# Convolution from stacked taps on half the array, softplus as one ScalarE activation, slots set anew

## The reference

```
xn = layernorm(x) * (1 + scale) + shift
x_in, z = split(xn @ in_proj_w.T)                  # 1024 channels each
u  = silu(causal_conv(x_in, 4 taps per channel) + conv_b)
dt_r, B, C = split(u @ x_proj_w.T)                 # 64, 16, 16
dt = softplus(dt_r @ dt_proj_w.T + dt_proj_b)
A  = -exp(A_log)
for t: h = h * exp(dt[t] * A) + (dt[t] * u[t]) * B[t];  y[t] = sum over 16 states of h * C[t]
y  = (y + u * D_param) * silu(z);   x + gate * (y @ out_proj_w.T)
```

## Time and profile before

| | |
|---|---|
| median of 3 runs (lowest to highest) | 2305.18 us (2304.23 to 2309.43) |
| profiled execution, its own time | 2300.15 us |
| its span, mean granted TensorE clock | 2298.4 us, 0.964 |
| busy PE, DVE, ACT, POOL | 2129.7, 2043.7, 1607.3, 1776.1 us |
| first scan to last scan | 65.5 to 1804.6 us |
| chunks 1 to 7, length | 215.9, 216.6, 218.1, 215.5, 218.4, 218.0, 214.3 us |

### The profile page before, as it was taken

One profiled execution on the slowest core, in us unless ns is written; L12 is line 12 of the kernel. 1 busy time (PEld: TensorE's weight loads), 2 busy tenths in 40 slices (PEclk: granted clock), 3 DMA queues, 4 the chain that ended last, 5 costly groups with the idle time before them and its releaser, 6 DMA issues. The chain is left out here.

```text
span 2298.4 us, 30570 instructions
## 1 busy us (share of the span) xinstructions
PE 2129.7 (93%) x10240; PEld 1396.4 (61%) x10240; DVE 2043.7 (89%) x2255; ACT 1607.3 (70%) x3120; POOL 1776.1 (77%) x1047
## 2 busy tenths in 40 slices
PE   8789989988998999899979988998977899999999
PEld 3355555555655555555545555555545588888878
DVE  4999999999999999999999999999999766666666
ACT  4677877887787778777877887777656355566655
POOL 0697899999999999999999999999999521233325
PEclk9999999999998999999999999998978999999999
DMA  7611321151114111421331141114001201121113
GB/s 241 244 38 51 123 103 47 53 177 46 51 51 166 51 55 43 179 92 51 115 111 47 51 165 56 42 53 173 33 28 53 93 28 35 33 63 60 40 56 129
DMA packets 86138, 191.20 MB, mean 83 GB/s; under 512 B 8349, under 2 KB 11677, under 8 KB 85982
## 3 DMA queue, kind: packets, MB, share of 16 engines
q1 hardware_dynamic: 85982, 189.25, 24.8%
HBM read 171.91 MB, written 17.30 MB: 82 GB/s over the span
## 5 line engine op out<-in xcount | busy, mean ns | idle before, releaser
L1473 POOL TENSOR_TENSOR arena<-arena 128x1024 f32<-128x1024 f32 x512 | 1201.2, 2365 | 114.4 <-ACT arena L628 112.0
L1065 DVE TENSOR_TENSOR_SCAN arena<-ps,arena 128x512 f32<-128x512 f32 x1024 | 1240.1, 1257 | 15.2 <-ACT ps L628 12.4
L628 ACT ACTIVATE ps<-arena 128x512 f32<-128x512 f32 x1087 | 717.3, 676 | 274.3 <-DVE arena L1065 188.1
L341 PEld LDWEIGHTS ps<-keep,arena 128*128 128x128 f32 x4096 | 491.2, 147 | 266.2 <-POOL arena L1473 133.6
L341 PE MATMUL ps<-keep,arena 128*128 128x128 f32 x4096 | 548.5, 284 | 98.0 <-POOL arena L1473 91.7
L1050 DVE TENSOR_TENSOR arena<-ps,arena 128x1024 f32<-128x1024 f32 x407 | 491.0, 1206 | 25.9 <-PE ps L341 23.4
L280 PE MATMUL ps<-arena 128*128 128x512 f32 x1024 | 469.3, 604 | 18.4 <-issue 17.6
L280 PEld LDWEIGHTS ps<-arena 128*128 128x128 f32 x1024 | 189.8, 195 | 219.9 <-issue 219.4
L628 ACT ACTIVATE arena<-ps 128x512 f32<-128x512 f32 (+1 forms) x393 | 198.4, 538 | 124.9 <-PE ps L280 64.4
L1440 POOL TENSOR_TENSOR arena<-arena 128x1024 f32<-128x1024 f32 x105 | 248.0, 2362 | 15.1 <-PE ps L341 15.1
L628 ACT ACTIVATE arena<-arena 128x2 f32<-128x2 f32 (+4 forms) x662 | 238.3, 365 | 26.4 <-POOL arena L1417 7.5
(11 more groups left out here) (151 smaller groups left out, 2693.6 us busy)
## 6 DMA issues: line engine op xcount, KB each, us to landing
arena<-scr_bc SPq DMA_DIRECT2D x128, 512.0 KB, 7.2
arena<-in_inT SPq DMA_DIRECT2D x184, 256.0 KB, 2.7
arena<-in_x SPq DMA_DIRECT2D x17, 512.0 KB, 3.8
scr_x<-arena SPq DMA_DIRECT2D x32, 256.0 KB, 2.0
arena_b<-scr_x SPq DMA_DIRECT2D x16, 512.0 KB, 3.6
arena_c<-scr_x SPq DMA_DIRECT2D x32, 256.0 KB, 2.9
out<-arena_c SPq DMA_DIRECT2D x32, 256.0 KB, 2.1
arena<-in_x SPq DMA_DIRECT2D x30, 256.0 KB, 3.4
```

The source lines that it names most:

```text
L341: last = e.matmul(YP[:, 128 * q:128 * q + 128], hb[G % R][:, i, 128 * q:128 * q + 128], ident, start=(g == 0 and i == 0 and q == 0), stop= ...
L628: return e.activation(o_, i_, f, **kw)
L1065: e.tensor_tensor_scan(H, DA[s % 4], H, h0, MUL, ADD).then_inc(v_sc)
L1473: e.tensor_tensor(H, H, Ct[:, GN * g:GN * g + GN, :], MUL).then_inc(g_w)
```

## The change

- **Convolution.** `xq` (two buffers of 516 columns) becomes `xt`, one buffer of 2 x 516 columns for the two halves h of a 128-channel block. Rows of half h hold its 64 channels; the other 64 rows hold the same channels one step later. `x_evac` writes only the first (four ACT instructions on 64 partitions in place of two on 128), and a new `shift` on SP copies them by two DMAs of 64 x 514 elements into the other rows. `conv_mm` waits for these (`d_sh`) and then has four matmuls of 64 columns, two halves h by two pairs of taps p, the halves on different columns of the array. `x_evac` waits for the convolution just before, as there is one buffer.
- **Step size.** `softplus` is one activation, Softplus, followed by a preload of the table set of Exp. `add` is gone; `du` waits for `softplus` and stands at slot 5. At the start DVE's sum of the two parts (line 1118) is gone.
- **Slots.** `POOLED` has 19 groups in eight units where the code had 15 (the words of the change say 13): 133 in all for 105. The tables of slots are new.

```diff
-        xq, _ = [sb(516) for _ in range(2)], sb(504)
+        xt, _ = sb(2, 516), sb(504)
...
-        AT = {"dt": 4, "soft": 6, "add": 5, "du": 8, "copy": 12, "yt": 6, "yb": 9, "yf": 13, "proj": (6, 14), "xdbl": (7, 4)}
-        XMM = {(3, 0): 0, (3, 7): 1, (3, 15): 2, (4, 6): 3, (5, 1): 4, (5, 3): 5, (5, 15): 6, (6, 1): 7}
-        XEV = {(3, 4): 0, (3, 10): 1, (4, 2): 2, (4, 11): 3, (5, 4): 4, (5, 5): 5, (6, 2): 6, (6, 5): 7}
-        CMM = {(3, 5): 0, (3, 12): 1, (4, 5): 2, (4, 13): 3, (5, 5): 4, (5, 8): 5, (6, 5): 6, (6, 11): 7}
+        AT = {'dt': 4, 'soft': 6, 'du': 5, 'copy': 12, 'yt': 6, 'yb': 9, 'yf': 11, 'proj': (7, 1), 'xdbl': (7, 4)}
+        XMM = {(3, 0): 0, (3, 4): 1, (4, 0): 2, (4, 5): 3, (4, 13): 4, (5, 4): 5, (6, 1): 6, (6, 4): 7}
+        XEV = {(3, 4): 0, (3, 8): 1, (4, 2): 2, (4, 9): 3, (4, 15): 4, (5, 7): 5, (6, 3): 6, (6, 8): 7}
+        SHIFT = {after(k, 1): i for k, i in XEV.items()}
+        CMM = {(3, 5): 0, (3, 11): 1, (4, 5): 2, (4, 12): 3, (5, 1): 4, (5, 9): 5, (6, 4): 6, (6, 9): 7}
...
-        ZSILU = {(1, 15): (1, 2), (4, 1): (0,), (5, 1): (0,), (6, 0): (0,), (6, 11): (1,), (7, 15): (1, 2)}
+        ZSILU = {(1, 15): (1, 2), (4, 0): (0,), (5, 1): (0,), (6, 1): (0,), (6, 15): (1,), (7, 15): (1, 2)}
...
-        OUTA = {(1, 4): 0, (1, 12): 1, (2, 10): 2, (2, 15): 3}
+        OUTA = {(0, 13): 0, (1, 10): 1, (2, 9): 2, (3, 2): 3}
...
-        pooled = lambda U, g: U > 6 and U != 39 and g in ((1,), (1, 3), (1, 3), (1, 3), (1,), (0, 1, 3), (1, 3), (1, 3))[U % 8]
+        pooled = lambda U, g: U > 6 and U != 39 and g in ((0, 1, 3), (1, 3), (1, 2, 4), (1, 3), (0, 2), (0, 3, 5), (0, 3, 5), (1,))[U % 8]
...
             def conv_mm(c, i):
                 no = 8 * (c - 1) + i
-                e.wait_ge(a_xh, no + 1)
-                e.wait_ge(a_xq, no + 1)
+                e.wait_ge(d_sh, 32 * (no + 1))
...
-                for w in range(4):
-                    last = e.matmul(P, W[:, w, :], X[:, w:w + T], start=(w == 0), stop=(w == 3))
+                for p in range(2):
+                    for h in range(2):
+                        last = e.matmul(P[64 * h:64 * h + 64, :], W[:, 2 * h + p, 0:64], xt[:, h, 2 * p:2 * p + T],
+                                        start=(p == 0), stop=(p == 1))
...
             def x_evac(c, i):
...
-                if no >= 2:
-                    e.wait_ge(p_w, c_no((no - 2) // 8 + 1, (no - 2) % 8) + 1)
+                if no:
+                    e.wait_ge(p_w, c_no((no - 1) // 8 + 1, (no - 1) % 8) + 1)
...
-                act(X[:, 3:T + 3], P, ACT.Identity).then_inc(a_xq)
+                for h in range(2):
+                    rows_ = slice(64 * h, 64 * h + 64)
+                    act(xt[rows_, h, 3:T + 3], P[rows_, :], ACT.Identity).then_inc(a_xq)
...
             def softplus(U):
...
-                act(spt, BG[bank_of["dt", U]], ACT.Abs).then_inc(a_abs)
...
-                if U:
-                    act(dt[U % 2], BG[bank_of["dt", U]], ACT.Relu).then_inc(a_rl)
-                e.wait_ge(a_abs, U + 1)
-                act(spt, spt, ACT.Exp, scale=-1.0).then_inc(a_ex)
-                e.wait_ge(a_ex, U + 1)
-                act(spt, spt, ACT.Ln, bias=1.0).then_inc(a_ln)
+                act(dt[U % 2], BG[bank_of["dt", U]], ACT.Softplus).then_inc(a_sp)
+                e.preload_act_table_set("natural_log_exp_and_others")
...
-            def add(U):
-                e.wait_ge(a_ln, U + 1)
-                e.tensor_tensor(dt[U % 2], dt[U % 2], spt, ADD).then_inc(g_dt)
...
+            def shift(no):
+                e.wait_ge(a_xh, 2 * no + 2)
+                e.wait_ge(a_xq, 2 * no + 2)
+                for h in range(2):
+                    to, of = slice(64 * (1 - h), 64 * (1 - h) + 64), slice(64 * h, 64 * h + 64)
+                    e.dma_start(xt[to, h, 0:T + 2], xt[of, h, 1:T + 3]).then_inc(d_sh, 16)
```

More of the change, by code:

```diff
@@ L127, in program @@
         d_x1 = [sem(f"d_x1{i}") for i in range(2)]
-        d_rows = sem("d_rows")
+        d_rows, d_sh = sem("d_rows"), sem("d_sh")
         d_X = [sem(f"d_X{i}") for i in range(4)]
@@ L137, in program @@
             ("ft", "q", "v", "k", "qt", "kt", "kv", "ya", "o"))
[L139 to L141 removed]
+        a_sc, a_A, a_row, a_no, a_xn, a_xh, a_hi, a_e0, a_xq, a_ue, a_du, a_su, a_xd, a_sp, a_sz, a_da, a_st, a_dg, a_x1, a_sm, a_sq = (
+            sem("a_" + n) for n in ("sc", "A", "row", "no", "xn", "xh", "hist", "e0", "xq", "ue", "du", "su", "xd", "sp", "sz",
+                                    "da", "st", "dg", "x1", "sm", "sq"))
         a_wh, a_nx, a_f, a_fh, a_qe, a_qT, a_ek, a_E, a_fc = (sem("a_" + n) for n in ("wh", "nx", "f", "hi", "qe", "qT", "ek", "E", "fc"))
@@ L323, in dt_mm @@
                 e.wait_ge(a_xd, c + 1)
-                P = bank(("dt", U), (a_rl, U) if U else (v_0, 2), 16 * (U - 1) + AT["soft"] + 2 if U else None)
+                P = bank(("dt", U), (a_sp, U + 1), 16 * (U - 1) + AT["soft"] + 2 if U else None)
                 e.matmul(P, wdt[0:65, 128 * j:128 * j + 128], xdbl[c % 2][0:65, :], start=True, stop=True).then_inc(p_dt)
@@ L766, in exps @@
                 if n == 0:
-                    e.wait_ge(*((g_dt, U) if U else (v_0, 2)))
+                    e.wait_ge(a_sp, U + 1)
                 if s >= 4:
@@ L802, in _ @@
             silu_u(0, 7, 8)
-            e.preload_act_table_set("natural_log_exp_and_others")
+            e.preload_act_table_set("softplus")
             proj_evac(0)
@@ L1044, in expand @@
                 if g == 0:
-                    e.wait_ge(*((a_du, U) if U else (v_0, 3)))
+                    e.wait_ge(*((a_du, U) if U else (v_0, 2)))
                 if U % 8 == 0:
@@ L1454, in _ @@
                 more = c + 1 < NCH
-                if U + 1 < NU and pr == AT["add"]:
-                    add(U + 1)
                 if U + 1 < NU and pr == AT["du"]:
@@ L1641, in _ @@
                     load_C(c, g)
+                if more and (j, pr) in SHIFT:
+                    shift(8 * c + SHIFT[j, pr])
                 if (j, pr) in XMM and more:
@@ L1754 @@
     one[64, 0] = 1.0
-    taps = np.zeros((8, 128, 4, 128), np.float32)
-    taps[:, range(128), :, range(128)] = a["conv_w"].reshape(8, 128, 4).transpose(1, 0, 2)
+    taps, m, cw = np.zeros((8, 128, 4, 128), np.float32), np.arange(64), a["conv_w"].reshape(8, 2, 64, 4)
+    for h in range(2):
+        for p in range(2):
+            taps[:, 64 * h + m, 2 * h + p, m] = cw[:, h, :, 2 * p]
+            taps[:, 64 * (1 - h) + m, 2 * h + p, m] = cw[:, h, :, 2 * p + 1]
     parts = {
```

40 lines of the change are left out of this document (18 added, 22 removed).

## The result

The changed kernel takes **2279.80 us** (median of 4 runs, 2277.18 to 2283.83) for 2304.70 before (2303.77 to 2309.43, run beside it): a ratio of **0.9895, 95% interval 0.9875 to 0.9916**, 24.9 us less. The profiled execution took 2282.22 us with a span of 2280.4, 17.9 less than the one of before. Of the 17.9, 15.3 lie ahead of the end of the last scan (1804.6 before, 1789.2 now) and 2.6 behind it, in the attention layer, which the change leaves as it is; why that part is shorter is not shown.

A forecast was written before the change was run, and what follows sets the result against it. DVE was taken to bound the kernel, with POOL and PE close behind. DVE -31, PE -12 and ACT +21 sum to -22 us: 2278 against the profiled execution, 2283 against the median, range 2257 to 2304.

The forecast's parts named there:

- What bounds: In a chunk after the change, DVE falls from 212 to 207 us, POOL stays about 206, ACT is at 83%.
- DVE, -31: 28 outer products leave DVE for POOL, each worth 1.11 us on the path: -31 us.
- The start, nothing: Removing DVE's sum at the start gains nothing, since the first outer product waited for the DMA of B until 64.17.
- POOL, nothing: POOL gets 66 us of outer products, loses 71 us of `add`s, and its waits shrink: counted at nothing.
- ACT, +68 us of work and +21 on the path: Softplus's table loads add net 68 us to ACT; 1 us shows at three spots in each of 7 chunks: +21.
- PE, -12: Convolutions of about 2.1 us for 3.60, less 60 us of DMA waits; half of DVE's 24 us waits for PE go.
- `du_copy`: ACT's 27.6 us wait behind POOL's `du` is shortened, as `du` comes three slots sooner; supports ACT's small price.
- A: Softplus's loads stall DVE's scans in every unit, 63 us in place of 21: about 2325; chance 0.09.
- B: POOL becomes the bound at 215.5 us a chunk, only 10 us gained: 2295; chance 0.13.
- C: PE's relief and the new slots remove DVE's waits and ACT adds none: 2254; chance 0.08.
- D: Column tiles do not run side by side or `shift` is late; PE at 223 us a chunk: about 2345; chance 0.05.
- E: A table load holds ACT twice as long when sets alternate often, 145 us more: about 2325; chance 0.02.

The follow-up runs named there:

- the extra sum: The changed kernel with one more 128 x 504 sum on POOL in each unit, just ahead of `du`, which nothing waits for: 2310.35 us.
- unit 40's groups: The changed kernel with pooled groups 0 and 1 of unit 40 made on DVE again: 2279.51 us alone.

## Why the prediction was right, step by step

The forecast was 2283 and the time 2279.8; the sum against the profiled execution was -22, its profile shows -17.9. The mechanism was right: DVE's work falls, and a part comes back as waits. The terms held less evenly. DVE's scans in the whole kernel, before and with the change, with the idle time in front of them:

```profile
L1065 DVE TENSOR_TENSOR_SCAN arena<-ps,arena 128x512 f32<-128x512 f32 x1024 | 1240.1, 1257 | 15.2 <-ACT ps L628 12.4 <-POOL arena L1440 2.4
L1060 DVE TENSOR_TENSOR_SCAN arena<-ps,arena 128x512 f32<-128x512 f32 x1024 | 1234.2, 1247 | 31.1 <-ACT ps L630 19.7 <-POOL arena L1433 10.2 <-issue 0.5
```

- **What bounds.** DVE and POOL level at 207 and 206 of a chunk, ACT at 83%: 207.43, 205.25 and 84%. Right.
- **DVE, -31.** 379 outer products are left, and their busy time fell from 491.0 to 453.5 us. Put back alone, the list costs 15.3: the other half was spent again on waits, as the sum foresaw with its +21, though for POOL as well as for ACT.
- **The start, nothing.** The first outer product came at 64.99 for 64.17 and waited for B. Right.
- **POOL, nothing.** This term failed. DVE's wait for POOL went from 2.4 to 10.2 us, and the extra sum (+30.6) shows that POOL's work reaches the path much as DVE's does. That POOL's load was unchanged was right; that its bunched groups would cost nothing was not. The run with groups moved out of unit 0 got 9.6 us back, with unit 40's groups in it. The wait of `du` shrank as forecast: its idle time is 15.9 us, where `add` had 31.2.
- **ACT, +68 us of work and +21 on the path.** By groups ACT gained 75 us, and its busy time, the union, 98: two `exps` of 0.68 us overlap to 1.30, while nothing overlaps the loads at 570.89 and 572.80. The block is 3.21 us for 3.2. DVE's wait for ACT rose by 7.3 us over the kernel (12.4 to 19.7) and not to the 30 that I named as a sign. The spots were right: units 2, 5 and 6 have 7.9, 4.2 and 6.4 of the 19.7 us, 0.9 us each time. But units 2 and 5 had 10.6 us before the change already, so only a third of the 21 came on. With POOL's 7.8 the price of both is 15. So the 21 was a fair size for the whole and too large for ACT alone.
- **PE, -12.** The convolution takes 1.94 us for 2.1, the landing 2.3 us for 2.5, and the waits come to 20 us where I had 60: `conv_mm` stands far enough behind `x_evac` at most places. DVE's wait for PE fell by 7.0 (23.4 to 16.4), and the old convolution alone costs 10.6. Right in sign and nearly in size.
- **`du_copy`.** The 27.6 us that ACT waited for POOL's `du` are gone from the list of its waits, and the 19.3 for convolutions fell to 1.3.

The sum with these values: -31 for DVE (taken over, not measured by itself), -7 for PE, +7 for ACT, +8 for POOL, +1 at the start, -22. That it is the forecast's own -22 is luck in part: ACT was priced 14 us too high, POOL 8 and PE 5 too low, and this cancels. The profile's 17.9 leaves 4 us. Two terms stand where I had not looked: DVE's product with the gate at the end of a unit (line 1081, 1086 before) now waits 6.2 us for PE where it waited 1.2, and the attention layer is 2.6 us shorter. With them the sum is -20, and 2 us stay open. Two more things were not in the sum, the 219.5 us of chunk 5 and that the new list of groups depends on the new softplus through `spt` (95 us without it).

**The rivals.** A (ACT's lead gone everywhere) did not come: DVE had 31 waits for ACT in the 56 units from 290 to 1790 us, 0.6 us each, where A has 1.0 in every unit. B came in part, as above, but chunks are 214 us and not 215.5. C did not come: its 2254 lies 26 us below the time, and even with one group a chunk moved and unit 40's put back the kernel takes 2270. D is refuted for the change, with 1.94 us and 20 us of waits. A convolution of 3.6 us with `shift` ran at 2339 us, near D's 2345, but not by D's path: PE was busy there for 206 of the 222 us of chunk 3, where D had 223 and PE above the chunk. E is refuted: the 240 loads took 1283 ns in the mean, and the activation behind the load at 570.89 began 1.30 us after it. The Trainium skill ("ScalarE: Activation LUTs", "What ACT_TABLE_LOAD costs") adds a drain of 1380 ns to each switch; this trace does not show one, with at least two switches in every unit.

## What to carry to other kernels

When two engines are level, work moved from one to the other can give back much less than its own time, here half (15.3 of 31 us), and then it counts where the moved pieces stand: one group a chunk, taken from the unit where POOL is late to one where it isn't, was worth, with unit 40's groups, nearly as much (9.6 us) as the whole new convolution (10.6). A scratch buffer that two engines share is a term of the sum: look for who else reads it before costing a shorter producer. And before halving a matmul with column tiles, price the copy that they need by its landing and by the slots between producer, copy and consumer, and not by its bytes.
